# Moving a small piece of row arithmetic from VectorE to ScalarE and GpSimd, with a new order for four engines

## The reference

```python
mod = (silu(c) @ wmod).reshape(8, 6, 1, 128)
sa, ca, ga, sb, cb, gb = (mod[:, k] for k in range(6))
ga = (2 * (ga >= 0) - 1) * maximum(abs(ga), 0.25)
gb = (2 * (gb >= 0) - 1) * maximum(abs(gb), 0.25)
h = layernorm(x) * (1 + ca) + sa
x = x + ga * attn(h)        # per sequence: rank the 256 tokens by a score, work on the better 128,
                            # (projection, gating, top-2 of 8 experts), put them back
h = layernorm(x) * (1 + cb) + sb
out = x + gb * ffn(h)       # fp4(silu(fp4(h) @ w_gate') * (fp4(h) @ w_up')) @ w_down', all fp4-rounded
```

## Time and profile before

| what | value |
|---|---|
| median of 3 runs | 245.74 us |
| the profiled execution | 245.69 us |
| span of its instructions | 243.9 us |
| PE busy | 218.0 us (89%) |
| DVE busy | 200.7 us (82%) |
| ACT busy | 131.7 us (54%) |
| POOL busy | 72.6 us (30%) |
| share of the last-ending chain | DVE 40%, PE 32%, issue 11%, ACT 8% |

### The profile page before, as it was taken

One profiled execution on the slowest core, in us unless ns is written; L12 is line 12 of the kernel. 1 busy time (PEld: TensorE's weight loads), 2 busy tenths in 40 slices (PEclk: granted clock), 3 DMA queues, 4 the chain that ended last, 5 costly groups with the idle time before them and its releaser, 6 DMA issues.

```text
span 243.9 us, 4519 instructions
## 1 busy us (share of the span) xinstructions
PE 218.0 (89%) x1431; PEld 176.6 (72%) x1436; DVE 200.7 (82%) x667; ACT 131.7 (54%) x343; POOL 72.6 (30%) x92
## 2 busy tenths in 40 slices
...
DMA packets 9126, 12.01 MB, mean 49 GB/s; under 512 B 1184, under 2 KB 5256, under 8 KB 9104
## 3 DMA queue, kind: packets, MB, share of 16 engines
...
## 4 chain that ended last, share of the span: by engine, by line
DVE 40%; PE 32%; issue 11%; ACT 8%; POOL 4%; DMA 3%; SPq 1%; DVEq 0%; ACTq 0%; POOLq 0%
PE down_ps L1076 14%; PE up_ps L1076 9%; PE aux_ps L1076 8%; DVE acc L993 4%; DVE q_am L760 3%; DVE stats L730 3%; DVE qa L773 3%; POOL rstd L505 2%; ACT perm_m L604 2%; DMA wmod_s<-wmod_dram 2%; ACT h1T L669 2%; DVE hx L836 2%; DVE hh L1049 2%; DVE hh L1045 2%; DVE hx L829 2%
## 5 line engine op out<-in xcount | busy, mean ns | idle before, releaser
L669 ACT ACTIVATE h1T<-up_ps,par 128x256 f32<-128x256 f32 (+1 forms) x160 | 58.1, 434 | 40.8 <-PE up_ps L1076 32.6
L1076 PE MATMUL down_ps<-w_s,h1T 128*128 128x128 f32 x512 | 67.8, 280 | 5.2 <-DVE acc L993 4.3
L1076 PEld LDWEIGHTS down_ps<-w_s,h1T 128*128 128x128 f32 x512 | 63.5, 194 | 11.8 <-issue 9.9
L1076 PE MATMUL up_ps<-n2T,w_s 128*128 128x256 f32 (+1 forms) x320 | 66.3, 342 | 2.0 <-ACT h1T L669 2.0
L1076 PEld LDWEIGHTS up_ps<-n2T,w_s 128*128 128x128 f32 x320 | 49.7, 192 | 8.8 <-issue 4.9
L505 POOL TENSOR_TENSOR rstd<-veps,half_pow 128x2 f32<-128x2 f32 (+3 forms) x17 | 14.9, 875 | 83.9 <-DVE veps L735 83.9
L993 DVE SCALAR_TENSOR_TENSOR acc<-down_ps,gate,acc 128x128 f32<-128x128 f32 x64 | 20.2, 346 | 8.6 <-PE down_ps L1076 8.0
L1076 PE MATMUL aux_ps<-w_guT,h2T 128*128 128x352 f32 x64 | 21.4, 460 | 0.0
L1076 PE MATMUL up_ps<-lower,ones_b 128*128 128x512 bf16 x76 | 18.9, 379 | 0.5 <-issue 0.3
L558 ACT ACTIVATE qb<-qa 128x704 f32<-128x704 f32 (+5 forms) x20 | 11.3, 569 | 14.3 <-DVE qa L764 14.3
L543 POOL DMA_INDIRECT out_dram<-yo,row_ix x16 | 16.2, 1011 | 5.4 <-issue 2.4
...
## 6 DMA issues: line engine op xcount, KB each, us to landing
...
mod_r<-mod_dram SPq DMA_DIRECT2D x1, 768.0 KB, 4.7
...
```

The costliest lines, as they stand in the source:

```text
L669: last = A.activation(h1T[:, m % 2, hc, 0:n], up_ps[j % UP_BANKS][:, h * n:(h + 1) * n], ACT.Gelu, bias=col("moe_b1", e * HC + hc))
L1076: return nc.tensor.matmul(o, lhsT=l, rhs=r, start=start, stop=stop)
```

## The change

ACT takes over the copy of the result of `mod.0.1` out of PSUM, and POOL the arithmetic behind it. POOL does it in 11 instructions, 10 of them in two chains of five in which each waits for the one before; DVE did it in 10 with the copy. A semaphore, mod_step, is added for POOL's chain. All four order strings are replaced; apart from `mod.0.1` and the `spare` steps, they hold the same steps as before.

```diff
@@ POOL's loop
+                elif kind == "mod":
+                    wait_aux_taken(pool, kind, a, i, 0)
+                    step_no = 0
+                    v = mod_s[:, CB * D:(CB + 1) * D]
+                    nc.gpsimd.tensor_scalar(v, v, 1.0, None, ALU.add)
+                    for m in (GA, GB):
+                        v, sign, size = mod_s[:, m * D:(m + 1) * D], mod_t[:, 0, :], mod_t[:, 1, :]
+                        nc.gpsimd.tensor_scalar(sign, v, 0.0, 2.0, ALU.is_ge, ALU.mult).then_inc(mod_step, 1)
+                        pool.wait_ge(mod_step, step_no + 1)
+                        nc.gpsimd.tensor_scalar(sign, sign, -1.0, None, ALU.add).then_inc(mod_step, 1)
+                        pool.wait_ge(mod_step, step_no + 2)
+                        nc.gpsimd.tensor_tensor(size, sign, v, ALU.mult).then_inc(mod_step, 1)
+                        pool.wait_ge(mod_step, step_no + 3)
+                        nc.gpsimd.tensor_scalar(size, size, 0.25, None, ALU.max).then_inc(mod_step, 1)
+                        pool.wait_ge(mod_step, step_no + 4)
+                        last = nc.gpsimd.tensor_tensor(v, sign, size, ALU.mult)
...
+                    last.then_inc(mod_ready, 1)
@@ ACT's loop
+                elif kind == "mod":
+                    wait_aux_full(act, kind, a, i, 0)
+                    A.activation(mod_s[:, GA * D:], aux(kind, a, i, 0)[0:B, :], ACT.Copy
+                                 ).then_inc(aux_taken(kind, a, i, 0), 1)
@@ DVE's loop
-                    else:
-                        V.tensor_copy(mod_s[:, GA * D:], src[0:B, :]).then_inc(aux_taken(kind, a, i, 0), 1)
-                        wait_aux_taken(dve, kind, a, i, 0)
-                        v = mod_s[:, CB * D:(CB + 1) * D]
-                        V.tensor_scalar(v, v, 1.0, None, ALU.add)
-                        for m in (GA, GB):
-                            v = mod_s[:, m * D:(m + 1) * D]
-                            V.tensor_scalar(mod_t[:, 0, :], v, 0.0, 2.0, ALU.is_ge, ALU.mult)
-                            link(V.scalar_tensor_tensor(mod_t[:, 1, :], v, -1.0, v, ALU.mult, ALU.max))
-                            link(V.tensor_scalar(mod_t[:, 1, :], mod_t[:, 1, :], 0.25, None, ALU.max))
-                            last = V.scalar_tensor_tensor(v, mod_t[:, 0, :], -1.0, mod_t[:, 1, :], ALU.add, ALU.mult)
...
-                        last.then_inc(mod_ready, 1)
@@ the order strings, the first line of two of them
-modh.0.0 mod.0.0-1 modh.0.1 spare.23.0 hT.0.0 spare.3.1 hr.0.0 wT.0.0 spare.1.2 srow.0.0 spare.4.3 scol.0.0
+modh.0.0-1 mod.0.0-1 spare.9.0 hT.0.0 spare.3.1 hr.0.0 wT.0.0 spare.1.2 srow.0.0 wM.0.0 scol.0.0 spare.16.3
-rsh.0.0 rsh.1.0 rsh.2.0 rs1.0.0 rs2.0.0 rs1.1.0 gather.1.0 gather.0.0-2 gather.1.1 gather.0.3 rs1.2.0 rs2.1.0
+rsh.0.0 mod.0.1 rsh.2.0 rsh.1.0 rs1.0.0 gather.0.0 rs2.0.0 rs1.1.0 gather.1.0 gather.0.1 gather.1.1 gather.0.2-3
```

More of the change, by code:

```diff
@@ L76 @@
[L76 to L78 removed]
+modh.0.0-1 mod.0.0-1 spare.9.0 hT.0.0 spare.3.1 hr.0.0 wT.0.0 spare.1.2 srow.0.0 wM.0.0 scol.0.0 spare.16.3
+place.0.0 spare.2.4 hT.1.0 spare.3.5 hr.1.0 perm.0.0-1 srow.1.0 spare.4.6 scol.1.0 spare.1.7 n1.0.0 spare.3.8
@@ L79 @@
 """
 DVE_ORDER = """
[L82 to L86, removed]
```

99 lines of the change are left out of this document (53 added, 46 removed).

## The result

The changed kernel takes 245.03 us (median of 20 runs, 244.06 to 246.41), the kernel before 246.14 us measured beside it (20 runs, 245.19 to 248.31). The ratio is 0.9946, with a 95% interval of 0.9925 to 0.9967: 1.3 us faster. The forecast was 243.6 us against 245.69, a ratio of 0.9915. The direction and the range held, and the size was too large: by 0.8 us if ratios are compared (0.0031 of 246), by 1.4 us if times are.

What follows compares the result with a forecast made beforehand. It took PE as nearly full from 42 to 220 us, DVE setting the pace before and after. Span 243.9 - 1.3 - 2.0 - 1.7 + 2.0 - 2.0 + 2.9 = 241.8, with 1.8 outside 243.6 us; range 240.9 to 247.0.

Steps and rivals of the forecast that it cites:

- The start, -1.3: Head of the kernel: DVE loses mod.0.1 (2.77 us), waits 1.8 us at lnB.1, and the first up comes 1.3 us earlier.
- ScalarE and GpSimd, 0: Moved modulation: ACT's copy costs nothing, POOL's chain takes 4.4 us of the 7.6 it may take before anything waits.
- The rival of a dear chain: POOL's chain at 1.05 us an instruction makes lnC.1 wait 3.9 us: 247.5 us, chance 0.05.
- the shared access: DVE and POOL excluding each other in SBUF: 1.6 us over lnC.0's four instructions, swallowed by the wait at lnB.1.
- The passage, -2.0 and -1.7: Passage to the experts: PE's 2.0 us wait for a gelu goes, and the low clock behind it, worth 1.7 us.
- New waits of PE, +2.0: Expert stretch: DVE's new order makes PE wait 4.9 us at three steps, partly offset by idle time; net 2.0 us lost.
- rival three: The change does nothing that counts: low clock comes elsewhere, the start's gain is lost waiting for rows; 245.8 us, chance 0.10.
- The end, -2.0 and +2.9: Tail: PE steps moved behind the last down save 2.0 us; DVE steps moved behind the last acc cost 2.9 us.

Runs made afterwards that it cites:

- e2: The kernel before with only mod.0.1 moved to ScalarE and GpSimd, the other orders as before: 245.91 us, ratio 0.9998 to the kernel before.
- e3: e2 with lnA.2 and wbc of VectorE ahead of lnA.1 and lnB.1, and rsh.2 ahead of rsh.1 on GpSimd: 246.35 us, ratio 1.0008.
- e10: e3 with 9 spare products of TensorE ahead of hT.0 in place of 23: 243.42 us, ratio 0.9894 to the kernel before.
- e1: The changed kernel with mod.0.1 put back on VectorE, the new orders kept: 249.88 us, ratio 1.0164 to the kernel before.
- e7: e3 with TensorE's and ScalarE's orders up to the first scol as in the changed kernel (9 spare products): 243.48 us, ratio 0.9902.
- e12: e7 with ScalarE's expc.0 and tanh.1 ahead of the first gelu: 242.75 us, ratio 0.9878 to the kernel before.
- e13: e12 with TensorE's place.2 ahead of up.0.2: 242.65 us, ratio 0.9856 to the kernel before.
- e9: The changed kernel with three output row buffers in place of two, each with its semaphore: 244.16 us, ratio 0.9935 to the kernel before.
- e5: The changed kernel with TensorE's n1.2 behind up.0.12 and up.0.13: 244.62 us, ratio 0.9954 to the kernel before.
- e6: The changed kernel with 18 spare products of TensorE in place of 10 behind dn.4.0: 244.64 us, ratio 0.9926 to the kernel before.

## Why the prediction was right in sign and too large in size

*The start, -1.3.* Right in mechanism, too small: 2.15 us at the first `up`. `lnB.0` at 7.98 (8.2 said). The rows landed near 15.1, not 16.3, so `lnB.1` waited 0.75 us and not 1.8. In the twelve profiles that have the move it started between 14.6 and 16.1. What I did not see is the condition for this term: lnA.2 ahead of the wait and the filler of 9 in place of 23. With neither (e2) 0.08 us arrived, with the first alone (e3) nothing, with both (e10) 2.5 us; the second alone was not run. My working had lnA.2 in its sum ahead of `lnB.1`, without saying that the gain hung on it; the filler it did not have.

*ScalarE and GpSimd, 0.* Right, with less room than said: the chain took 6.7 us and not 4.4, of the 7.6 allowed. The rival of a dear chain (1.05 us an instruction) fell. For the shared access: `lnC.0` took 1.14 us, as before; only its last instruction lay beside the chain. The rule of the Trainium skill ("SBUF — State Buffer", "SBUF: two separate sides"), by which the prediction put a loss at 1.6 us, had little to act on there. `lnB.1` lay beside the chain and the start of the root behind it, and took 1.65 us, against 1.14 in before and 1.13 in e1, which has no chain. The eight instructions of `lnB.0` and `lnB.1` in the changed kernel (shortest, median and longest in ns):

```profile
L838 DVE SCALAR_TENSOR_TENSOR hx<-hx,mv,mod_r x8: 329/337/585, 8.0 to 16.2; 128x128 f32<-128x128 f32 x8
```

The four of `lnB.1` took 511, 443, 340 and 585 ns, where e1's took 345 to 348. So a loss exists, half a microsecond over four instructions and not one GpSimd instruction each (0.44 to 0.65 us). Over the twelve profiles that have the chain, `lnB.1` took 1.33 to 1.73 us.

*The passage, -2.0 and -1.7.* The step that failed. The wait for the gelu and the low clock behind it did go. But I priced them on TensorE, the engine with the highest busy share, and there they were not on the path. For the low clock e3 and e7 show it: both have before's orders in the passage and the same wait of 1.94 us for the gelu, and only e3 has the low clock behind it (e3 first):

```profile
50.50:53.90 3.40, 3.40 (x14) 3.04 (x13) 2.43 (x11) 3.36 (x8) 0.00 (x0) 0.50 0.07 19
40.00:54.00 14.00, 11.28 (x74) 9.71 (x73) 10.27 (x47) 13.87 (x33) 5.52 (x6) 1.00 0.11 30
```

From `scol.0` to `acc.0.0` e3 takes 42.91 us and e7 42.93: the 1.7 us were worth nothing. The runs of the kernel before agree. Of the 81 measured beside the experiments, the 51 with a mean clock of 0.985 to 0.989 have a median of 245.65 us, and the 14 with 0.994 to 0.997 one of 246.45, so a higher clock there went with no shorter time. For the wait the evidence is less direct: in e12 it is longer (2.56 us), and `acc.0.0` comes 0.3 us sooner than in e7. ScalarE's own chain sets this stretch (ScalarE of e7; three table loads lie between 43.9 and 50.6, two are shown):

```profile
43.90 1.28 ACT L698 ACT_TABLE_LOAD   x1
45.20 1.57 ACT L698 ACTIVATE h1T<-up_ps,par 128x256 f32<-128x256 f32 x4
46.78 1.28 ACT L640 ACT_TABLE_LOAD   x1
48.08 0.21 ACT L640 ACTIVATE e_col<-d_col 128x4 f32<-128x4 f32 x1
```

and VectorE waits for it: 2.34 us ahead of `yA.1`. e12 and e13 together took that idle time away and got 2.2 us from `scol.0` to `acc.1.0`, in a place where I had said the table loads were worth nothing more.

*New waits of PE, +2.0.* PE's idle time between first `up` and last `down` went from 8.7 to 9.3 us with the 2.0 for the gelu gone, so 2.6 came new; the 1.7 at `n1.2` is the largest but one. In its own book the term was near. Of its three waits, PE stood 1.8 us behind `acc.1.2` (1.9 said), 0.55 at `gateT.1` (1.8 said) and 1.7 at `n1.2` (1.2 said). On the path the wait at `n1.2` cost nothing (e9, e5): VectorE has no gap over 0.6 us from 45 to 109 us in the changed kernel.

*The low clock is not a place but a risk.* I counted it as gone with the wait before it. It came back behind `n1.2` (0.57 for 4 us) and in the tail, for 0.6 us each on the path; in e1 and e6 it came ahead of `acc.1.3`, for 1.6 us. What decides where it comes, in one program from run to run, stays open. That is rival three, which I gave 0.10, and it holds in part.

*The end, -2.0 and +2.9.* The tail from the last `down` took 27.6 us (27.2 said), with 0.56 of low clock in it. The last `down` ended at 215.6 (214.6 said). e7 gives the sum: against it, the changed kernel has the last acc 2.5 us earlier and 4.2 us more from there to `yo.7` (21.31 against 17.09). From 112 us on PE is busy for 99.6 of 103.7 us and VectorE idle for 20.3: the moved steps lay free there, and behind the last acc each is paid. Without low clock the exchange is even. From `scol.0` to the last acc e5 takes 198.1 us and e7 201.8, and from there to `yo.7` 20.8 and 17.1: 3.7 us gained and 3.7 lost. The changed kernel's loss of some 1.2 us against e7 and e10 is low clock. The 13 runs of e7 and e10 show none that costs time, which doesn't say that before's orders are safe from it: the kernel before, nine times in 81, took 247.6 to 249.2 us at clocks of 0.977 to 0.979.

By the book of times: predicted -2.1 us of span, measured -0.7. The start gave 0.85 us more than said, the stretch up to the last `down` 1.85 less (-1.85 in place of -3.7), and the end cost 0.4 more. In the 1.85 are 0.6 us of low clock behind `n1.2`; the other 1.25 no run divides among the terms, but the 1.7 put on the low clock of the passage, worth nothing, is more than that. The 0.4 at the end is the 0.56 of low clock there. That the total came out within 1.4 us is in part luck, since the start's 0.85 hid part of the passage. Two things stay open: why e1 had low clock in all its six runs (mean 0.963 to 0.978), and why one of its last transfers took 1.0 us longer.
